# Layer norm in a two-half transformer kernel: the power of minus one half on GpSimd tile by tile in four instructions, and VectorE's centring tile by tile behind it

## What is computed

```python
def _layernorm(x, axis=-1, eps=1e-05):
    m = jnp.mean(x, axis=axis, keepdims=True)
    v = jnp.var(x, axis=axis, keepdims=True)
    return (x - m) / jnp.sqrt(v + eps)

x = x + 0.5 * _L0_ffn_ref(_layernorm(x), ...)    # low-rank feed-forward with gelu
x = x + _L0_attn_ref(_layernorm(x), ...)         # 16 causal softmax heads, then one more layer norm, Wo
x = x + 0.5 * _L0_ffn_ref(_layernorm(x), ...)
x = x + 0.5 * _L1_ffn_ref(_layernorm(x), ...)    # shared expert and 8 routed experts, top 2
x = x + _L1_attn_ref(_layernorm(x), ...)         # 16 heads of second-order Taylor attention
x = x + 0.5 * _L1_ffn_ref(_layernorm(x), ...)
```

## Time and profile before

| | |
|---|---|
| median of three runs | 1515.85 us (1515.03 to 1517.44) |
| the profiled execution: its own time | 1510.05 us |
| its span from first to last instruction | 1508.2 us |
| TensorE matmuls busy | 1238.7 us, 82% of the span |
| TensorE weight loads busy (beside the matmuls) | 686.2 us, 45% |
| VectorE busy | 1078.3 us, 71% |
| ScalarE busy | 750.7 us, 50% |
| GpSimd busy | 308.1 us, 20% |
| data moved by DMA | 28.77 MB, mean 19 GB/s |

### The profile page before, as it was taken

The page is one execution under the profiler, slowest core; times in us unless marked ns, Lnnn a source line. Parts: engine busy times, 40 slices in busy tenths (PEclk is TensorE's granted clock), DMA queues, the critical chain, the costliest instruction groups (busy, mean ns, idle before and its releaser), DMA issues. The chain is left out here.

```text
span 1508.2 us, 27324 instructions
## 1 busy us (share of the span) xinstructions
PE 1238.7 (82%) x10040; PEld 686.2 (45%) x10064; DVE 1078.3 (71%) x3235; ACT 750.7 (50%) x1246; POOL 308.1 (20%) x807
## 2 busy tenths in 40 slices
PE   5698659987798887888789877898778888898886
PEld 2354235444443454434454344544455345553544
DVE  6985368667886678866778658876687767866756
ACT  3166336652466425664276533765337653454442
POOL 1024001331014200242002420133101331122220
PEclk9699669999999989999889998999989999999999
DMA  3100000100010000100001000010000100101000
GB/s 115 43 2 1 7 22 15 29 8 22 8 33 12 8 22 8 43 2 10 27 1 43 8 10 20 1 43 8 21 9 3 42 1 5 46 1 43 2 1 14
DMA packets 37205, 28.77 MB, mean 19 GB/s; under 512 B 7961, under 2 KB 36305, under 8 KB 37073
## 3 DMA queue, kind: packets, MB, share of 16 engines
q1 hardware_dynamic: 37072, 27.04, 6.7%
HBM read 5.90 MB, written 2.10 MB: 5 GB/s over the span
## 5 line engine op out<-in xcount | busy, mean ns | idle before, releaser
L772 ACT ACTIVATE left<-bank 128x512 f32<-128x512 f32 x280 | 159.8, 600 | 84.3 <-PE bank L1242 81.4
L962 DVE TENSOR_REDUCE left<-bank 128x4 f32<-128x512 f32 x280 | 184.5, 683 | 23.1 <-PE bank L1223 21.7
L814 ACT ACTIVATE right<-bank 128x512 f32<-128x512 f32 x280 | 158.4, 601 | 85.6 <-PE bank L1329 79.0
L1165 PE MATMUL bank<-right,pairs 128*128 128x512 f16 x588 | 160.9, 397 | 23.7 <-DVE right L1041 17.1
L1221 PE MATMUL bank<-left 128*128 128x512 f16 (+1 forms) x448 | 128.5, 336 | 59.8 <-DVE left L952 28.5
L1092 DVE TENSOR_SCALAR right<-right 128x1024 f32<-128x1024 f32 x168 | 105.5, 654 | 62.0 <-ACT right L814 61.4
L1062 DVE SCALAR_TENSOR_TENSOR right<-bank,right 128x128 f32<-128x128 f32 x448 | 126.1, 344 | 30.6 <-PE bank L1305 23.9
L1355 PE MATMUL bank<-right 128*32 128x256 f32 (+3 forms) x1792 | 133.1, 435 | 0.0
L1305 PE MATMUL bank<-ew,right 128*128 128x128 f32 x896 | 119.3, 278 | 9.8 <-ACT right L791 6.0
L1305 PEld LDWEIGHTS bank<-ew,right 128*128 128x128 f32 x896 | 113.4, 191 | 29.8 <-DVE right L1062 11.5
L684 POOL TENSOR_TENSOR spareB<-neghalf 1x1 f32<-1x1 f32 x192 | 47.7, 249 | 327.9 <-DVE right L1092 252.5
(11 more groups left out here) (280 smaller groups left out, 2287.4 us busy)
## 6 DMA issues: line engine op xcount, KB each, us to landing
right<-right SPq DMA_DIRECT2D x168, 64.0 KB, 2.1
left<-left SPq DMA_DIRECT2D x168, 32.0 KB, 1.9
left<-x_dram SPq DMA_DIRECT2D x7, 256.0 KB, 2.8
out_dram<-right SPq DMA_DIRECT2D x7, 256.0 KB, 2.3
left<-left SPq DMA_DIRECT2D x24, 64.0 KB, 2.1
right<-right SPq DMA_DIRECT2D x24, 32.0 KB, 1.9
wo<-wo_dram SPq DMA_DIRECT2D x1, 512.0 KB, 3.2
ew<-ew_dram SPq DMA_DIRECT2D x1, 512.0 KB, 4.6
```

What stands on the lines that cost most here:

```text
L772: act.activation(h.probs[:, g % 2, u * S:(u + 1) * S], ps[:, :], ACT.Exp).then_inc(h.act, 1)
L814: act.activation(h.wts[:, p % 2, u * S:(u + 1) * S], ps[:, :], ACT.Square, bias=1.0, scale=FEAT ** -0.5).then_inc(h.act, 1)
L962: dve.tensor_reduce(h.bmax[:, u * NT:(u + 1) * NT], ps[:, :].rearrange("p (b k) -> p b k", k=P), AX.X, ALU.max).then_inc(h.dve, 1)
L1165: done = mm(out, left, right, start=first, stop=last)
```

## The change

```diff
@@ ln_scale, GpSimd @@
                 pool.wait_ge(h.vare_ready, it * h.lns + k + 1)
-                pool.tensor_tensor(h.rstd[:, :], h.vare[:, :], neghalf[:, :], ALU.pow).then_inc(h.rstd_ready, 1)
+                for t in range(NT):
+                    pool.tensor_tensor(h.rstd[:, t:t + 1], h.vare[:, t:t + 1], neghalf[:, t:t + 1], ALU.pow)\
+                        .then_inc(h.rstd_ready, 1)
@@ centre, VectorE @@
                 src = h.attn if h in (A1, A2) and k == 2 else h.x
-                dve.wait_ge(h.rstd_ready, it * h.lns + k + 1)
                 for t in range(NT):
+                    dve.wait_ge(h.rstd_ready, (it * h.lns + k) * NT + t + 1)
                     last = dve.tensor_scalar(h.ln[:, t, :], src[:, t, :], h.mv[:, t, 0:1], h.rstd[:, t:t + 1],
                                              ALU.subtract, ALU.mult)
                 last.then_inc(h.ln_ready, 1)
```

## The result

The change makes the kernel slower: 1531.76 us in the median of four runs (1527.07 to 1532.67) against 1515.44, a ratio of 1.0108 with a 95% interval of 1.0075 to 1.0141. Measured again beside the experiments it gave 1529.37 us in the median of six runs, a ratio of 1.0093 (1.0075 to 1.0111). The profiled execution took 1531.92 us, 21.9 more than the profiled one of before.

A forecast was written before the change was run, and what follows sets the result against it. No engine is full; chains passing from engine to engine set the time. Per turn -0.9 - 0.31 + 0.46 = -0.75 us, -6.0 in eight turns' worth, times 0.7 is -4.2: 1511.7 us, range 1505 to 1560.

The forecast's parts named there:

- R2: Rival: a one-column power costs 0.6 us, 2.7 us a turn lost, 1531 us in all; chance 0.14.
- the prediction's formula: Sum over a turn's seven norms: -0.75 + 12 x (price of a one-column power - 0.39) us; sign changes at 0.45.
- (a): Norm where masks slow the centrings and TensorE waits 1.76 us; early centrings mostly escape the masks, -0.9 us.
- (b): Norm where VectorE waits 1.41 us for the root, then TensorE 0.37; centring ends earlier, -0.31 us.
- (c): Norm where TensorE reaches its transposes 0.36 us after the centrings are done; 0 on TensorE, 0.23 us of VectorE's time.
- (d): Norm with masks right behind the power, for which TensorE's denominators wait 0.61 us; later end of powers costs +0.46 us.
- (e): Norm whose power runs beside four pad instructions of VectorE; TensorE waits 0.47 us; centring ends about as before, 0.
- (g): Norm where VectorE waits 0.24 us and TensorE's transposes follow at once without a wait; claimed 0.
- The 0.7 let through: Estimated share of the -6.0 us over 56 norms that reaches the end, giving -4.2 us.
- The added waits at nothing: VectorE's three added waits per norm priced at nothing; at 0.04 us each it would be 0.1 us a norm.
- R4: Rival: powers and centrings get in each other's way, 2.2 us a turn lost, 1528 us; chance 0.13.
- (f): Norm where VectorE begins to centre 2.4 us after the power's end; claimed 0.

The follow-up runs named there:

- the tail: Kernel before, plus GpSimd powers and adds over 1 to 16 columns after everything is stored; a one-column power took 0.55 us, whole time not compared.
- the run with (d) alone: Against the kernel before: four one-column powers only in the left half's second attention-batch norm, added waits everywhere; 1527.58 us, ratio 1.0066.
- idle powers: Kernel before, plus two unused one-column powers behind the one power on GpSimd in all 56 norms; 1520.66 us, ratio 1.0023.

## Why the prediction was wrong

It forecast 1511.7 us and a gain; it is 1531.76 and a loss, inside the range, on the side of its rival R2 (a price between, 1531 us for 0.6 us a power). That R2's figure comes out to the microsecond is luck: its price is too high and its share let through too small, and it has no term for the clock.

*The step that failed is the price of a one-column power.* The prediction took 0.39, because "it looks like one long computation run once for each column, which leaves little for a fixed part". The trace could not show it; the tail showed 0.155 us a column and 0.21 us fixed beyond the add. Its own turning point was 0.45 us, only 0.06 above the value taken, and the measured 0.55 lies beyond it. With 0.55 the prediction's formula, -0.75 + 12 x 0.16, gives +1.2 us a turn where 1.59 was measured.

*The places.* The mechanism of each was right, with 0.55 in the place of 0.39:
- (a): the early centrings do escape the masks. It was to be -0.9; the last root is 0.6 later than at 0.39, so TensorE's wait falls by 0.29 only.
- (b): three starts at 0.52, the last power's 0.55, 0.03 and a centring of 0.35 make 2.49 us where it was 2.17: +0.33, for -0.31.
- (c): nothing, as said; the 0.36 us of slack just covers it.
- (d): +1.10, for +0.46. This is 8 us of the 13, and the run with (d) alone shows it.
- (e): +0.13 and (g) +0.32, for 0. The formula treated them as free at any price near 0.39, but (g) had no slack behind its centrings: TensorE's wait there is 0.26 us in four of the five turns (0.18 in the last), where it was 0.

*The 0.7 let through was too small.* The steps of (b), (c), (d) and (e) are the same in all five turns to 0.02 us apart from the clock, and 1.59 x 8 = 12.7 agrees with +13.1 and +12.5 at equal clock, so about all of it reached the end and a share near 1.0 would have fitted. With 0.7 the formula gives +6.6 us.

*The added waits at nothing* is not refuted: the ratio leaves 0 to 5.8 us for them, and the step at (b) is 0.06 us. *R4* is refuted by the centrings beside idle powers. The Trainium skill's page "SBUF — State Buffer", section "Who interferes with whom", has the later of two block fully for the whole instruction of the first, where VectorE is in a mode with two ports, which it allows for such instructions. Here centrings that start after a power has started are not slowed (0.35 us each), and in the change, where VectorE pauses between them, the powers keep their 0.55 too. The measurement decides against that rule for the power. The prediction's own reason, that a power holds the way only where it reads and writes, rested on the 1.21 us at (e); it stays an inference, as that power took 1.01 us elsewhere beside the same instructions. For masks the blocking is borne out, but not its order: in (d) of the change the last centring starts at 712.88 and takes 0.92 us, and the masks that start behind it, at 712.95 and 713.31, take 0.40 each as always.

*What was not in the prediction* is the granted clock. It is 0.0038 lower, which at 0.61 us a thousandth goes with 2.3 us of the difference of the means, 15.4 us (1530.8 of four runs less 1515.4). The two profiled executions stand further apart (21.9 us) because the one of before ran at 0.945, well above its own mean of 0.939, and the one of after at 0.934.

## What to carry to other kernels

Before cutting one instruction into n to let a consumer start early, find its fixed cost, not only its duration: the last piece comes n - 1 fixed costs later, and that must be less than the consumer's work that is hidden. Here four pieces paid 3 x 0.37 us and hid 3 x 0.26; two paid 0.37 and hid 2 x 0.26, which was too little to measure. Then look behind the producer in its own queue: over half of the loss came at one place in seven, where masks behind the powers fed TensorE, which no figure of the producer and its consumer shows.

## What the runs showed of the hardware

**A power on GpSimd** costs 0.40 us and 0.155 us for a column of 128 partitions. At 16 columns it is 2.9 us where an add is 0.22.

**A power can give way to VectorE, and doesn't always.** Two idle powers of 1.07 us lasted 2.77 beside the plus-one on VectorE, whose centrings before it kept 1.11 for four. The second of them ended 0.04 us after the last plus-one. The power of place (e), started 0.03 us before the same four pad instructions each time, took 1.21 us in one run and 1.01 in another. A mask on GpSimd does slow the centrings.

**The granted clock can take another course at the same place.** Stretches of 2 us from the same part of a turn, just before place (f) and behind it, first in the kernel before, then in the changed one. Columns: the stretch, its length, busy time (and instructions) of TensorE's matmuls, its weight loads, VectorE, ScalarE and GpSimd, then the granted clock as a share of full speed, DMA share, GB/s.

```profile
566.00:568.00 2.00, 0.38 (x4) 0.27 (x4) 1.97 (x7) 0.00 (x0) 0.00 (x0) 1.00 0.38 123
568.00:570.00 2.00, 0.67 (x8) 0.29 (x6) 1.88 (x9) 0.00 (x0) 1.09 (x2) 0.93 0.03 8
570.00:572.00 2.00, 0.81 (x4) 0.37 (x4) 1.95 (x7) 0.00 (x0) 0.12 (x1) 0.50 0.00 0
...
574.00:576.00 2.00, 2.00 (x10) 1.11 (x10) 1.04 (x6) 0.80 (x2) 0.00 (x0) 0.50 0.00 0
576.00:578.00 2.00, 1.33 (x18) 0.72 (x16) 1.88 (x7) 1.86 (x3) 0.00 (x0) 0.86 0.01 2
```

```profile
572.70:574.70 2.00, 0.40 (x4) 0.27 (x4) 1.97 (x7) 0.00 (x0) 0.00 (x0) 1.00 0.41 124
574.70:576.70 2.00, 0.73 (x7) 0.42 (x6) 1.87 (x9) 0.00 (x0) 1.10 (x3) 0.62 0.03 7
576.70:578.70 2.00, 0.83 (x6) 0.39 (x4) 1.96 (x7) 0.00 (x0) 1.49 (x3) 0.50 0.00 0
...
582.70:584.70 2.00, 1.67 (x18) 0.80 (x16) 1.88 (x7) 1.85 (x3) 0.00 (x0) 0.50 0.01 2
...
586.70:588.70 2.00, 2.00 (x6) 0.57 (x4) 0.00 (x0) 0.90 (x2) 0.00 (x0) 0.50 0.00 0
588.70:590.70 2.00, 1.42 (x6) 0.42 (x6) 1.84 (x3) 1.97 (x3) 0.00 (x0) 0.96 0.02 4
```

In both, TensorE has little to do for some time (0.38 to 0.83 us busy of each 2 us) and the clock falls to 0.50, that is from 2.4 to 1.2 GHz. The same work stands 6.7 us later in the changed kernel. Before, a mean of 0.93 in its stretch puts the fall at about 569.7, and the return, from the 0.86, at about 576.6: 7 us at the lower level. After the change the fall is at about 575.2, 1.2 us earlier in the sequence, and the return at about 588.9, 5.6 us later: 13.7 us. The step from this norm to the next is then +1.17, where the turn without that difference has +0.32.

One such pair doesn't show what the change does to the clock, as the turns of one kernel differ too: in the five turns the clock is at 0.50 for 10, 17, 20, 10 and 14 us before, and for 20, 20, 17, 20 and 24 us after.

In all the variants the mean clock came out between 0.9317 and 0.9367 (0.9157 for the slowest kernel), against 0.9391 in the kernel before with a standard error of 0.0006. Even the one with only the added waits, whose work is hardly shifted, has 0.9361. Why every variant has a lower clock, where chance would let some have a higher one, is left open.
